# A two-block transformer kernel whose linear-attention loop takes its last two sequences one at a time

## The chip, the cores and the metric

The kernel runs on one core of a Trainium2 chip. The metric is the device time of one launch in microseconds. TensorE multiplies matrices into PSUM banks, VectorE and ScalarE work on SBUF and PSUM, GpSimd on SBUF alone, and SyncE issues the DMAs of the weights and of the output. The engines run beside each other and wait for one another through semaphores.

## The reference

x has 16 sequences of 128 tokens and 128 features, all float32. The first block is a conditioned transformer layer (16 heads of 8 features, RoPE, softmax attention, a gated feed-forward layer). The second, which the change touches, is linear attention. Cut to what matters:

```
xn = layer_norm(x)                      # x: output of the first block
q, k, v = xn@Wq+bq, xn@Wk+bk, xn@Wv+bv  # 16 heads of 8
q = softmax(q over the 8 features of a head)
k = softmax(k over the 128 tokens)
y = q @ (k^T v)  per head
h = layer_norm(y)*g*(1+scale)+shift     # scale, shift from cond
out = x + cond * (silu(h)@out_W + out_b)
```

Each sequence is independent of the others in the second block, so how many go together is free.

## The kernel before, in words

The first block works on sequences one by one (attention, to about 128 us) and then on pairs (feed-forward). UNIT is 2, U is 8, and `pair(u)` is the slice of pair u. The second block is a pipeline written out by hand: each engine has a function or loop body for a step t, and in step t it works on several pairs at different depths (`u = t - 3`, `u = t - 6` and so on). There are CD_STEPS = U + 9 steps. The order of the instructions of one engine in a step is the order of its program, each with waits on semaphores that count pairs. An engine never passes a waiting instruction, and buffers are doubled by `u % 2`.

The names that follow are used for the instructions; a number in brackets is the pair (or part).

- GpSimd (`blocks_gpsimd`), in its order in a step: qs (L509, q minus its maximum), res (L514, the result, for `t - 8`), then for `t - 5` nmr (L519, pairs below DRAIN alone), var (L481) and the power rstd (L483, in `std`) and nmr again (L523), then xs3 (L528, x times its inverse deviation, for t).
- ScalarE (`blocks_scalar`): kx (L580, two exponentials), qvb (L589, copy of q and v), qxT (L599), qe (L605), hT4 (L536, two, modulated layer norm of y) and th (L613, tanh), kxT (L618), xs4 (L624, two, normalised y, below DRAIN alone).
- VectorE (`c_step` in `blocks_vector`): qrec (L687), qmax (L693), hs (L699, for `t - 6`), bn (L705, two, for `t - 4`), krec (L711), mv (L716, two), cx (L723, two, for `t - 3`), xs (L733, two, for `t - 4` and from pair DRAIN on), gated (L742, output times cond, for `t - 6`), hT (L748), kmax (L752), qsum (L757), knb (L762), y (L768, for `t - 3`).
- TensorE (`c_step` in `blocks_tensor`): ctx (L852, k^T v, for `t - 3`), xd (transposes of xs, `t - 5`), qe transposed (`t - 3`), out (L875 and L876, output projection, `t - 6`), xc (transposes of xs3, t), K (L892), Y (L901, `t - 3`), kT (transposes of kx, `t - 2`), QV (L920, L921, for t). All transposes go through a helper at L786.
- SyncE (L964 to L967): for each pair one store of 128 KB after res, then a wait for all.

DRAIN is U - 2 = 6, so xs of pairs 6 and 7 is made by VectorE, which waits for the power of the same pair. kT and out share PSUM bank 0. Two waits keep them apart, in TensorE's program:

```
e.wait_ge(c_kxT, min(u + 4, U))   # before out(u)
wait(e, d_gated, u - 3)           # before kT(u)
```

Of the kernel before, what the change touches and what calls it, by code (L numbers as in the profile page):

```python
# [29 lines left out]
ACT = mybir.ActivationFunctionType  # L30
# [41 lines left out]
CD_STEPS = U + 9  # L72
# [19 lines left out]
def is_unit(u):  # L92
    return not isinstance(u, int) or 0 <= u < U


def dit_then_linear_attention(nc, x, cond, pos, norm1_w, qkv_w, q_norm_w, k_norm_w, proj_w, proj_b,
# [3 lines left out]
    with ctx:  # L100
# [339 lines left out]
        def blocks_gpsimd(g):  # L440
# [37 lines left out]
            def std(u, ready, mv, var, added, rstd, made):  # L478

                g.wait_ge(ready, u + 1)  # L480
                q.tensor_scalar(var[:, pair(u)], mv[:, pair(u), 1], 1.0, EPS1, ALU.mult, ALU.add).then_inc(added, 1)  # L481
                g.wait_ge(added, u + 1)
                q.tensor_tensor(rstd[:, pair(u)], var[:, pair(u)], minus_half[:, 0:UNIT], ALU.pow).then_inc(made, 1)  # L483

            def std2(u):
                if is_unit(u):
                    std(u, b_mv, mv2, var2, c_var, rstd2, c_rstd)
# [12 lines left out]
            for t in c_range():  # L500
# [5 lines left out]
                if is_unit(u):  # L506
                    g.wait_ge(c_qmax, u + 1)
                    wait(g, c_qe, u - 1)
                    q.tensor_tensor(qs[u % 2][:, :, :, :], qvb[u % 2][:, :, 0:D].rearrange("p u (h d) -> p u h d", d=DH),  # L509
                                    qmax[u % 2][:, :, :].unsqueeze(3).to_broadcast([128, UNIT, H, DH]), ALU.subtract).then_inc(c_qs, 1)  # L510
                u = t - 8
                if is_unit(u):
                    g.wait_ge(d_gated, u + 1)
                    q.tensor_tensor(res[:, pair(u), :], gated[u % 2][:, :, :], x2[:, pair(u), :], ALU.add).then_inc(s_res, 1)  # L514
                u = t - 5
                if is_unit(u):
                    g.wait_ge(c_mv, u + 1)
                    if u < DRAIN:
                        q.tensor_scalar(nmr3[:, pair(u)], mv3[:, pair(u), 0], -1.0, 0.0, ALU.mult, ALU.add)  # L519
                    std(u, c_mv, mv3, var3, d_var, rstd3, d_rstd)  # L520
                    if u < DRAIN:
                        g.wait_ge(d_rstd, u + 1)
                        q.tensor_tensor(nmr3[:, pair(u)], nmr3[:, pair(u)], rstd3[:, pair(u)], ALU.mult).then_inc(d_nmr, 1)  # L523
                u = t
                if is_unit(u):
                    g.wait_ge(c_rstd, u + 1)
                    wait(g, c_xsT, u - 1)
                    q.tensor_tensor(xs3[u % 2][:, :, :], x2[:, pair(u), :], wide(rstd2, u), ALU.mult).then_inc(c_xs, 1)  # L528

        def blocks_scalar(a, start=None):  # L530
# [39 lines left out]
            for t in c_range():  # L570
                u = t
                if u == 0:
                    a.wait_ge(c_xsT, u + 1)
                    q.activation(flat(hT3[u % 2]), bank[XC_BANK][:, 0:UNIT * T], ACT.Copy).then_inc(c_hT, 1)
                u = t - 2
                if is_unit(u):
# [7 lines left out]
                if is_unit(u):  # L584
# [4 lines left out]
                    q.activation(qvb[u % 2][:, :, 0:2 * D], bank[QV_BANK][:, :].rearrange("p (u f) -> p u f", f=2 * D),  # L589
                                 ACT.Copy).then_inc(c_qvb, 1)  # L590
                u = t
                if 0 < u < JOIN:
                    a.wait_ge(c_xsT, u + 1)
                    q.activation(flat(hT3[u % 2]), bank[XC_BANK][:, 0:UNIT * T], ACT.Copy).then_inc(c_hT, 1)
                u = t - 3
                if is_unit(u):
                    a.wait_ge(c_qxTp, u + 1)
                    wait(a, c_yp, u - 1)
                    q.activation(flat(qxT[u % 2]), bank[QT_BANK][:, 0:UNIT * T], ACT.Copy).then_inc(c_qxT, 1)  # L599
                u = t - 2  # L600
                if is_unit(u):
# [3 lines left out]
                    q.activation(qe[u % 2][:, :, :, :].rearrange("p u h d -> p (u h d)"),  # L605
                                 qs[u % 2][:, :, :, :].rearrange("p u h d -> p (u h d)"), ACT.Exp).then_inc(c_qe, 1)
                u = t - 5
                if is_unit(u):
                    a.wait_ge(d_xsT, u + 1)
                    wait(a, d_hs, u - 1)  # L610
                    modulated(hT4, u, u % 2, bank[XD_BANK], S3, A3).then_inc(d_hT, 1)
                    a.wait_ge(d_hT, u + 1)
                    q.activation(th4[u % 2][:, :], flat(hT4[u % 2]), ACT.Tanh, scale=0.5).then_inc(d_th, 1)  # L613
                u = t - 2
                if is_unit(u):
                    a.wait_ge(c_kxTp, u + 1)
                    wait(a, c_ctx, u - 1)
                    q.activation(flat(kxT[u % 2]), bank[KT_BANK][:, 0:UNIT * D], ACT.Copy).then_inc(c_kxT, 1)  # L618
                u = t - 4
                if is_unit(u) and u < DRAIN:  # L620
                    a.wait_ge(d_nmr, u + 1)
                    wait(a, d_xsT, u - 1)
                    for j in range(UNIT):
                        last = q.activation(xs4[u % 2][:, j, :], y[:, UNIT * u + j, :], ACT.Identity,  # L624
                                            bias=nmr3[:, UNIT * u + j:UNIT * u + j + 1], scale=rstd3[:, UNIT * u + j:UNIT * u + j + 1])
                    last.then_inc(d_xs, 1)

        def blocks_vector(v, start=None):
# [53 lines left out]
            def c_step(t):  # L682
                u = t - 3
                if is_unit(u):
                    v.wait_ge(c_qsum, u + 1)
                    wait(v, c_y, u - 1)
                    q.reciprocal(qrec[u % 2][:, :, :].rearrange("p u h -> p (u h)"),  # L687
                                 qsum[:, :, :].rearrange("p u h -> p (u h)")).then_inc(c_qrec, 1)
                u = t - 2
                if is_unit(u):  # L690
                    v.wait_ge(c_qvb, u + 1)
                    wait(v, c_qs, u - 1)
                    q.tensor_reduce(qmax[u % 2][:, :, :], qvb[u % 2][:, :, 0:D].rearrange("p u (h d) -> p u h d", d=DH),  # L693
                                    X_AXIS, ALU.max).then_inc(c_qmax, 1)
                u = t - 6
                if is_unit(u):
                    v.wait_ge(d_th, u + 1)
                    wait(v, d_op, u - 1)
                    q.scalar_tensor_tensor(hs[u % 2][:, :], th4[u % 2][:, :], 1.0, flat(hT4[u % 2]), ALU.add,  # L699
                                           ALU.mult).then_inc(d_hs, 1)  # L700
                u = t - 4
                if is_unit(u):
                    v.wait_ge(c_y, u + 1)
                    for j in range(UNIT):
                        last = q.bn_stats(bn3[:, UNIT * u + j, :], y[:, UNIT * u + j, :])  # L705
# [3 lines left out]
                if is_unit(u):  # L709
                    v.wait_ge(c_ctx, u + 1)  # L710
                    q.reciprocal(krec[:, :], ctx_[:, :, D:D + 1].rearrange("p u a -> p (u a)")).then_inc(c_krec, 1)  # L711
                u = t - 4
                if is_unit(u):
                    v.wait_ge(c_bn, u + 1)
                    for j in range(UNIT):
                        last = q.bn_aggr(mv3[:, UNIT * u + j, :], bn3[:, UNIT * u + j, :])  # L716
                    last.then_inc(c_mv, 1)
                u = t - 3
                if is_unit(u):
                    v.wait_ge(c_krec, u + 1)  # L720
                    wait(v, c_yp, u - 1)
                    for j in range(UNIT):
# [4 lines left out]
                if is_unit(u) and u >= DRAIN:  # L727
# [3 lines left out]
                    for j in range(UNIT):  # L731
                        b = UNIT * u + j
# [4 lines left out]
                if is_unit(u):  # L737
# [4 lines left out]
                    q.tensor_tensor(gated[u % 2][:, :, :], bank[OUT_BANK][:, 0:UNIT * D].rearrange("p (u f) -> p u f", f=D),  # L742
                                    gate[:, pair(u), :], ALU.mult).then_inc(d_gated, 1)
                u = t
                if is_unit(u) and u >= JOIN:
                    v.wait_ge(c_xsT, u + 1)
                    wait(v, c_k, u - 1)
                    q.tensor_copy(flat(hT3[u % 2]), bank[XC_BANK][:, 0:UNIT * T]).then_inc(c_hT, 1)  # L748
                u = t - 1
                if is_unit(u):  # L750
                    v.wait_ge(c_k, u + 1)
                    q.tensor_reduce(kmax[:, :], bank[K_BANK][:, 0:UNIT * T].rearrange("p (u t) -> p u t", t=T),  # L752
                                    X_AXIS, ALU.max, negate=True).then_inc(c_km, 1)
# [27 lines left out]
        def blocks_tensor(e, start=None):  # L781
# [61 lines left out]

            def c_step(t):
                u = t - 3
                if is_unit(u):
# [4 lines left out]
                    for j in range(UNIT):  # L851
# [4 lines left out]
                if is_unit(u):  # L856
# [4 lines left out]
                    turned(bank[XD_BANK], lambda j: xs4[u % 2][:, j, :], d_xsT)  # L861
                u = t - 3
                if is_unit(u):
                    e.wait_ge(c_qe, u + 1)
                    wait(e, c_qxT, u)
                    turned(bank[QT_BANK], lambda j: qe[u % 2][:, j, :, :].rearrange("p h d -> p (h d)"), c_qxTp)
                u = t - 6
                if is_unit(u):
# [3 lines left out]
                    e.wait_ge(c_kxT, min(u + 4, U))  # L872
                    for j in range(UNIT):
# [5 lines left out]
                if is_unit(u):  # L879
# [4 lines left out]
                    turned(bank[XC_BANK], lambda j: xs3[u % 2][:, j, :], c_xsT)  # L884
                u = t - 1
                if is_unit(u):
# [5 lines left out]
                    q.matmul(bank[K_BANK][:, 0:UNIT * T], linc[:, 2, :], flat(hT3[u % 2]), start=True, stop=True).then_inc(c_k, 1)  # L892
                u = t - 3
                if is_unit(u):
# [5 lines left out]
                    for j in range(UNIT):  # L900
# [3 lines left out]
                if is_unit(u):  # L904
# [5 lines left out]
                    turned(bank[KT_BANK], lambda j: kx[u % 2][:, j, :], c_kxTp)  # L910
                u = t
                if is_unit(u):
# [5 lines left out]
                    for j in range(UNIT):  # L918
# [1050 lines left out]
```

## Time and profile before

| | |
|---|---|
| runs | 212.53, 212.80, 213.04 us; median 212.8 |
| profiled execution | 211.97 us, span 210.2, mean granted clock 0.987 |
| busy (share of span) | TensorE 183.4 (87%), VectorE 164.0 (78%), ScalarE 130.7 (62%), GpSimd 135.9 (65%) |
| second block's loop | from about 161 us to the end |
| output | eight stores of 128.0 KB, median 1.8 us from issue to landing |

A timeline row gives the start in us from the span's start, the length in us, the engine, the line, the operation, the tile written and those read, the shapes and how many instructions were merged; in brackets how long the engine had been idle and who ended that. In the rows by stretch each engine has its busy time with the number of instructions, then come TensorE's granted clock (1.00 is 2.4 GHz, 0.50 is 1.2 GHz), the share of the DMA engines and GB/s; the order is TensorE's matmuls, its weight loads, VectorE, ScalarE, GpSimd. Consecutive starts on a full engine lie closer than the lengths, since the end of one overlaps the next.

### The profile page before, as it was taken

The page shows a single profiled execution, that of the slowest core. Times are in us where ns is not written, and L with a number is a line of the kernel's source. Part 1 is how long each engine was busy: PE and PEld are TensorE (multiplying, and loading weights), DVE is VectorE, ACT ScalarE, POOL GpSimd, SP SyncE. Part 2 cuts the span into 40 slices and gives each one's busy share as a digit, 9 for nine tenths or more (in the row PEclk, how much of TensorE's full clock was granted, in tenths as well). Part 3 has the DMA queues.
Part 4 walks back from the last instruction along what each step waited for, and adds up shares of the span by engine and source line. Part 5 has one row for each costly group of instructions (what it writes and reads, how often), then busy time and mean ns, then how long its engine had stood idle before and what let it go on. Part 6 is the DMA issues. An engine that isn't in the chain of part 4 may idle for free.

```text
span 210.2 us, 5867 instructions
## 1 busy us (share of the span) xinstructions
PE 183.4 (87%) x1986; PEld 141.1 (67%) x1986; DVE 164.0 (78%) x488; ACT 130.7 (62%) x354; POOL 135.9 (65%) x346
## 2 busy tenths in 40 slices
PE   1796868889999999899999999999998799998742
PEld 1544556667777777777776787788886478887522
DVE  4798898897979799996666434778899589999851
ACT  1476696677777777676555784453432367999740
POOL 8889798989786867758800783167512546757642
PEclk9999999999999999999999999999999999999995
DMA  5963000000000000000000000000000000001102
GB/s 111 280 178 142 0 5 3 0 0 3 3 3 2 3 6 0 3 3 2 3 3 0 3 3 0 2 0 0 6 0 0 0 2 3 0 25 30 51 26 74
DMA packets 9915, 5.13 MB, mean 24 GB/s; under 512 B 3025, under 2 KB 9758, under 8 KB 9758
## 3 DMA queue, kind: packets, MB, share of 16 engines
q1 hardware_dynamic: 6494, 4.08, 6.4%
q10 hardware_dynamic: 3392, 0.68, 1.6%
q8 instruction: 16, 0.26, 0.5%
q14 instruction: 13, 0.11, 0.2%
HBM read 3.71 MB, written 1.05 MB: 23 GB/s over the span
## 4 chain that ended last, share of the span: by engine, by line
PE 61%; DVE 21%; ACT 6%; issue 6%; POOL 2%; ACTq 2%; POOLq 0%; DVEq 0%
PE bank L1769 8%; DVE qkpad L1500 8%; PE bank L1778 7%; PE bank L1860 6%; PE bank L799 5%; PE bank L810 5%; PE bank L800 5%; PE bank L786 4%; PE bank L920 3%; PE bank L1801 2%; PE bank L1837 2%; PE bank L1872 2%; PE bank L852 2%; ACT probs L1201 2%; PE bank L1830 2%
## 5 line engine op out<-in xcount | busy, mean ns | idle before, releaser
L1201 ACT ACTIVATE probs<-bank 128x512 f32<-128x512 f32 x64 | 34.7, 594 | 22.6 <-PE bank L1778 22.5
L1500 DVE TENSOR_REDUCE qkpad<-bank 128x4 f32<-128x512 f32 x64 | 41.0, 684 | 9.1 <-PE bank L1769 7.7
L1778 PE MATMUL bank<-qTm,kBD 32*128 32x128 f32 x512 | 37.1, 283 | 0.4 <-ACT probs L1201 0.4
L1769 PE MATMUL bank<-kBD,qTs 32*128 32x256 f32 x224 | 31.7, 399 | 5.7 <-DVE qkpad L1500 4.2
L1778 PEld LDWEIGHTS bank<-qTm,kBD 32*128 32x128 f32 x512 | 31.0, 186 | 1.0 <-ACT probs L1201 0.6
L1769 PEld LDWEIGHTS bank<-kBD,qTs 32*128 32x128 f32 x224 | 19.8, 184 | 10.8 <-DVE qkpad L1500 7.4
L545 ACT ACTIVATE th<-bank 128x256 f32<-128x256 f32 x24 | 9.2, 384 | 18.9 <-PE bank L800 15.5
L1860 PE MATMUL bank<-probs,vpad 128*32 128x128 f32 x512 | 18.5, 277 | 0.2
L1051 POOL TENSOR_TENSOR partner<-qk,rope 128x96 f32<-128x96 f32 x32 | 14.3, 467 | 6.7 <-ACT qk L1243 6.7
L1801 PE MATMUL bank<-ident,qkpad 128*128 128x128 f32 x96 | 16.5, 281 | 0.8 <-DVE qkpad L1598 0.8
L481 POOL TENSOR_SCALAR var<-mv 128x2 f32<-128x2 f32 x16 | 3.1, 193 | 20.3 <-DVE mv L672 18.4
L1801 PEld LDWEIGHTS bank<-ident,qkpad 128*128 128x128 f32 x96 | 10.6, 141 | 7.2 <-issue 5.3
L1860 PEld LDWEIGHTS bank<-probs,vpad 128*32 128x32 f32 x512 | 12.6, 109 | 4.1 <-issue 2.0
L536 ACT ACTIVATE hT<-bank,mods 128x128 f32<-128x128 f32 x32 | 12.9, 459 | 2.9 <-PE bank L786 2.9
L799 PE MATMUL bank<-hT,w1T 128*128 128x256 f32 x48 | 14.5, 383 | 0.0
L1837 PE MATMUL bank<-qkvT,hT 128*128 128x384 f32 x32 | 14.5, 545 | 0.0
L800 PE MATMUL bank<-hT,w3T 128*128 128x256 f32 x48 | 14.3, 379 | 0.0
L810 PE MATMUL bank<-ff,w2T 128*128 128x256 f32 x48 | 12.9, 381 | 0.0
L786 PE MATMUL bank<-ident,xs 128*128 128x128 f32 x48 | 9.5, 280 | 3.0 <-DVE xs L733 1.8
L483 POOL TENSOR_TENSOR rstd<-var,minus_half 128x2 f32<-128x2 f32 x16 | 11.2, 699 | 1.3
L635 DVE SCALAR_TENSOR_TENSOR yg<-th,bank 128x256 f32<-128x256 f32 x24 | 10.0, 417 | 2.5 <-ACT th L545 2.2
L1062 POOL TENSOR_TENSOR rot<-qk,rope 128x256 f32<-128x256 f32 x16 | 11.6, 728 | 0.0
(250 smaller groups left out, 512.3 us busy)
## 6 DMA issues: line engine op xcount, KB each, us to landing
gate<-in_cond_dram SPq DMA_DIRECT2D x1, 1024.0 KB, 4.6
out_dram<-res SPq DMA_DIRECT2D x8, 128.0 KB, 1.8
xin<-in_x_dram ACTq DMA_DIRECT2D x2, 256.0 KB, 5.1
xin<-in_x_dram SPq DMA_DIRECT2D x1, 512.0 KB, 4.9
ada_n<-in_L_cond_ada_w_dram SPq DMA_DIRECT2D x1, 256.0 KB, 5.2
w_n<-in_L_cond_w_dram SPq DMA_DIRECT2D x2, 128.0 KB
qkv_n<-in_L_cond_qkv_w_dram SPq DMA_DIRECT2D x1, 192.0 KB, 3.9
w_n<-in_L_cond_w_dram SPq DMA_DIRECT2D x1, 170.5 KB
```

What stands on the lines that cost most here:

```text
L786: last = q.transpose(dst[:, j * 128:(j + 1) * 128], src(j), ident[:, :])
L799: q.matmul(bank[GU_BANK[c]][:, 0:UNIT * T], w1T[:, c * 128:c * 128 + 128], flat(hT2[1 - p]), start=True, stop=True)
L800: q.matmul(bank[GU_BANK[c]][:, UNIT * T:], w3T[:, c * 128:c * 128 + 128], flat(hT2[1 - p]), start=True, stop=True).then_inc(b_gu, 1)
L810: last = q.matmul(bank[F_BANK][:, 0:UNIT * T], w2T[:, c, :], ff[c][:, :], start=c == 0, stop=c == FC - 1)
L1051: last = q.tensor_tensor(heads(partner[b % 2][:, :, :])[:, :, :, k::2], heads(qk[b % NQK][:, :, :])[:, :, :, 1 - k:ROPE:2], table(b, 1)[:, ...
L1201: q.activation(probs[2 * r + i][:, :, :, :].rearrange("p f a t -> p (f a t)"), bank[E_BANK[i]][:, :], ACT.Exp, scale=SCALE).then_inc(s_p, 1)
L1500: q.tensor_reduce(out_, score_bank(b, r, i)[:, :].rearrange("p (f a t) -> p f a t", f=2, a=2), X_AXIS, ALU.max, negate=True).then_inc(s_ma ...
L1769: last = q.matmul(bank[S_BANK[i]][:, f * 2 * T:(f + 1) * 2 * T], qTs[b % 2][rows, f, :], kBD[b % NKB][rows, f, :, :].rearrange("p a t -> p ...
L1778: last = q.matmul(bank[E_BANK[i]][:, (2 * f + k) * T:(2 * f + k + 1) * T], kBD[t % NKB][rows, f, k, :], qTm[t % 2][rows, f, :], start=True ...
L1801: last = q.transpose(dst[:, at_ + f * T:at_ + (f + 1) * T], qkpad[b % NKB][:, s, 8 * f:8 * f + 8, :].rearrange("p h d -> p (h d)"), ident[ ...
L1837: q.matmul(front_bank(b)[:, 128:512], hT[b % 2][:, :], qkvT[:, :], start=True, stop=True).then_inc(s_qkv, 1)
L1860: last = q.matmul(bank[O_BANK][32 * c:32 * c + 32, r * T:(r + 1) * T], vpad[b % NVP][:, col:col + VSTEP], probs[2 * r + i][:, f, k, :], st ...
```

## The change

The second block's loop goes over nine parts in place of eight pairs. Parts 0 to 6 are the pairs 0 to 6; part 7 is sequence 14 alone and part 8 is sequence 15 alone. Each instruction of part 7 or 8 works on half the columns, groups of two instructions become one, and each of the two is stored by itself with 64 KB. There are 18 steps instead of 17. The offsets, the orders within a step, the banks and the buffers stay; DRAIN and JOIN keep their values, so parts 6, 7 and 8 have xs on VectorE. Everything ahead of the loop stays.

```diff
+C_UNITS = U + UNIT - 1
+CD_STEPS = C_UNITS + 9
+def is_part(u):
+    return not isinstance(u, int) or 0 <= u < C_UNITS
+def c_size(u):
+    return UNIT if u < U - 1 else 1
+def c_rows(u):
+    first = UNIT * u if u < U - 1 else UNIT * (U - 1) + u - (U - 1)
+    return slice(first, first + c_size(u))
...
-            def std(u, ready, mv, var, added, rstd, made):
+            def std(u, rows, ready, mv, var, added, rstd, made):
...
-                q.tensor_tensor(rstd[:, pair(u)], var[:, pair(u)], minus_half[:, 0:UNIT], ALU.pow).then_inc(made, 1)
+                q.tensor_tensor(rstd[:, rows], var[:, rows], minus_half[:, 0:rows.stop - rows.start], ALU.pow).then_inc(made, 1)
...
-                if is_unit(u):
-                    g.wait_ge(c_rstd, u + 1)
+                if is_part(u):
+                    g.wait_ge(c_rstd, min(u + 1, U))
...
-                if is_unit(u):
+                if is_part(u):
                     v.wait_ge(c_y, u + 1)
-                    for j in range(UNIT):
-                        last = q.bn_stats(bn3[:, UNIT * u + j, :], y[:, UNIT * u + j, :])
+                    for j in range(c_size(u)):
+                        last = q.bn_stats(bn3[:, c_rows(u).start + j, :], y[:, c_rows(u).start + j, :])
...
-                    e.wait_ge(c_kxT, min(u + 4, U))
-                    for j in range(UNIT):
+                    e.wait_ge(c_kxT, min(u + 4, C_UNITS))
+                    for j in range(c_size(u)):
...
                     wait(e, d_gated, u - 3)
-                    turned(bank[KT_BANK], lambda j: kx[u % 2][:, j, :], c_kxTp)
+                    turned_part(u, bank[KT_BANK], lambda j: kx[u % 2][:, j, :], c_kxTp)
...
-            for u in range(U):
+            for u in range(C_UNITS):
                 sp.wait_ge(s_res, u + 1)
-                sp.dma_start(out[pair(u), :, :].rearrange("b t f -> t b f"), res[:, pair(u), :]).then_inc(stored, 16)
-            sp.wait_ge(stored, 16 * U)
+                sp.dma_start(out[c_rows(u), :, :].rearrange("b t f -> t b f"), res[:, c_rows(u), :]).then_inc(stored, 16)
+            sp.wait_ge(stored, 16 * C_UNITS)
```

The other edits are of the same form: `is_unit` becomes `is_part`, `pair(u)` becomes `c_rows(u)`, a loop over UNIT becomes one over `c_size(u)`, and a tile is cut to its first `c_size(u)` entries.

## Rows read from the trace of the kernel before

**Rows 1.** Busy time by stretch; after the colon the length, then each engine.

```profile
187.30:191.00 3.70, 3.70 (x30) 3.31 (x29) 3.70 (x16) 3.67 (x12) 2.51 (x6) 1.00 0.13 40
202.00:206.00 4.00, 2.10 (x12) 1.57 (x12) 2.02 (x6) 1.23 (x3) 1.80 (x3) 0.84 0.11 33
```

**Rows 2.** VectorE's timeline, step 7; columns: start, length, line, operation, tiles, shapes.

```profile
187.12 0.41 DVE L748 COPY hT<-bank 128x256 f32<-128x256 f32 x1
187.45 0.41 DVE L752 TENSOR_REDUCE kmax<-bank 128x2 f32<-128x256 f32 x1
```

**Rows 3.** ScalarE's timeline, step 8.

```profile
190.21 0.38 ACT L599 ACTIVATE qxT<-bank 128x256 f32<-128x256 f32 x1
190.48 0.42 ACT L605 ACTIVATE qe<-qs 128x256 f32<-128x256 f32 x1
```

**Rows 4.** Groups by line and shape; count, then busy us and mean ns.

```profile
L1254 ACT ACTIVATE vpad<-bank 128x128 f32<-128x128 f32 x16 | 4.6, 288 | 0.0
...
L1519 DVE TENSOR_TENSOR o<-bank,rsum 128x128 f32<-128x128 f32 x16 | 4.5, 282 | 0.1
...
L1042 POOL TENSOR_TENSOR xs<-xin,rstd_x 128x128 f32<-128x128 f32 x8 | 3.2, 402 | 0.1
...
L483 POOL TENSOR_TENSOR rstd<-var,minus_half 128x2 f32<-128x2 f32 x16 | 11.2, 699 | 1.3
...
L1018 POOL TENSOR_TENSOR rstd_x<-ms,minus_half 128x4 f32<-128x4 f32 x2 | 2.0, 1025 | 0.5 <-DVE ms L1409 0.5
```

**Rows 5.** VectorE's timeline from mv(6) to the end.

```profile
196.88 0.23 DVE L716 BATCH_NORM_AGGREGATE mv<-bn 128x2 f32<-128x6 f32 x2
...
198.29 0.60 DVE L733 TENSOR_SCALAR xs<-y,mv,rstd 128x128 f32<-128x128 f32 x2 [0.68 <-POOL rstd L483]
198.81 0.42 DVE L742 TENSOR_TENSOR gated<-bank,gate 128x256 f32<-128x256 f32 x1
...
199.47 0.84 DVE L699 SCALAR_TENSOR_TENSOR hs<-th,hT 128x256 f32<-128x256 f32 x1
...
200.23 0.47 DVE L705 BATCH_NORM_STATS2 bn<-y 128x6 f32<-128x128 f32 x2
...
202.17 0.60 DVE L733 TENSOR_SCALAR xs<-y,mv,rstd 128x128 f32<-128x128 f32 x2 [1.18 <-POOL rstd L483]
...
204.41 0.42 DVE L742 TENSOR_TENSOR gated<-bank,gate 128x256 f32<-128x256 f32 x1 [0.97 <-PE bank L876]
204.75 0.41 DVE L699 SCALAR_TENSOR_TENSOR hs<-th,hT 128x256 f32<-128x256 f32 x1
...
206.79 0.42 DVE L742 TENSOR_TENSOR gated<-bank,gate 128x256 f32<-128x256 f32 x1 [1.63 <-PE bank L876]
```

**Rows 6.** GpSimd's timeline of the drain.

```profile
195.91 0.93 POOL L514 TENSOR_TENSOR res<-gated,x 128x256 f32<-128x256 f32 x1
...
197.27 0.19 POOL L481 TENSOR_SCALAR var<-mv 128x2 f32<-128x2 f32 x1 [0.43 <-DVE mv L716]
...
199.31 0.72 POOL L514 TENSOR_TENSOR res<-gated,x 128x256 f32<-128x256 f32 x1 [1.05 <-DVE gated L742]
...
207.30 0.72 POOL L514 TENSOR_TENSOR res<-gated,x 128x256 f32<-128x256 f32 x1 [1.55 <-DVE gated L742]
```

**Rows 7.** TensorE's timeline: ctx(7), first output matmuls of pairs 6 and 7.

```profile
196.05 0.71 PE L852 MATMUL bank<-qvb,kxT 128*128 128x129 f32 x4 [0.56 <-ACT kxT L618]
...
203.49 0.49 PE L875 MATMUL bank<-outw,hs 128*128 128x128 f32 x2 [0.22 <-DVE hs L699]
...
205.22 0.79 PE L875 MATMUL bank<-outw,hs 128*128 128x128 f32 x2 [0.85 <-DVE hs L699]
```

**Rows 8.** Busy time by stretch at the end, with granted clock and DMA share.

```profile
204.50:205.00 0.50, 0.00 (x0) 0.00 (x0) 0.50 (x2) 0.06 (x1) 0.09 (x1) 0.74 0.07 23
...
209.00:209.25 0.25, 0.00 (x0) 0.00 (x0) 0.00 (x0) 0.00 (x0) 0.00 (x0) 0.50 1.08 328
209.25:209.50 0.25, 0.00 (x0) 0.00 (x0) 0.00 (x0) 0.00 (x0) 0.00 (x0) 0.50 0.55 156
```

More of the change, by code:

```diff
@@ L511, in blocks_gpsimd @@
                 u = t - 8
-                if is_unit(u):
+                if is_part(u):
                     g.wait_ge(d_gated, u + 1)
-                    q.tensor_tensor(res[:, pair(u), :], gated[u % 2][:, :, :], x2[:, pair(u), :], ALU.add).then_inc(s_res, 1)
+                    q.tensor_tensor(res[:, c_rows(u), :], gated[u % 2][:, 0:c_size(u), :], x2[:, c_rows(u), :], ALU.add).then_inc(s_res, 1)
                 u = t - 5
-                if is_unit(u):
+                if is_part(u):
                     g.wait_ge(c_mv, u + 1)
@@ L609, in blocks_scalar @@
                     a.wait_ge(d_xsT, u + 1)
                     wait(a, d_hs, u - 1)
-                    modulated(hT4, u, u % 2, bank[XD_BANK], S3, A3).then_inc(d_hT, 1)
+                    rows = c_rows(u)
+                    for j in range(c_size(u)):
+                        b = rows.start + j
+                        last = q.activation(hT4[u % 2][:, j, :], bank[XD_BANK][:, j * T:(j + 1) * T], ACT.Identity,
+                                            bias=mods[:, b, S3:S3 + 1], scale=mods[:, b, A3:A3 + 1])
@@ L612, in blocks_scalar @@
+                    last.then_inc(d_hT, 1)
                     a.wait_ge(d_hT, u + 1)
-                    q.activation(th4[u % 2][:, :], flat(hT4[u % 2]), ACT.Tanh, scale=0.5).then_inc(d_th, 1)
+                    q.activation(th4[u % 2][:, 0:c_size(u) * T], flat(hT4[u % 2])[:, 0:c_size(u) * T], ACT.Tanh, scale=0.5).then_inc(d_th, 1)
                 u = t - 2
-                if is_unit(u):
+                if is_part(u):
                     a.wait_ge(c_kxTp, u + 1)
                     wait(a, c_ctx, u - 1)
-                    q.activation(flat(kxT[u % 2]), bank[KT_BANK][:, 0:UNIT * D], ACT.Copy).then_inc(c_kxT, 1)
+                    q.activation(flat(kxT[u % 2])[:, 0:c_size(u) * D], bank[KT_BANK][:, 0:c_size(u) * D], ACT.Copy).then_inc(c_kxT, 1)
@@ L619, in blocks_scalar @@
                 u = t - 4
-                if is_unit(u) and u < DRAIN:
+                if is_part(u) and u < DRAIN:
                     a.wait_ge(d_nmr, u + 1)
                     wait(a, d_xsT, u - 1)
-                    for j in range(UNIT):
-                        last = q.activation(xs4[u % 2][:, j, :], y[:, UNIT * u + j, :], ACT.Identity,
-                                            bias=nmr3[:, UNIT * u + j:UNIT * u + j + 1], scale=rstd3[:, UNIT * u + j:UNIT * u + j + 1])
+                    for j in range(c_size(u)):
+                        b = c_rows(u).start + j
+                        last = q.activation(xs4[u % 2][:, j, :], y[:, b, :], ACT.Identity,
+                                            bias=nmr3[:, b:b + 1], scale=rstd3[:, b:b + 1])
@@ L726, in c_step @@
                 u = t - 4
-                if is_unit(u) and u >= DRAIN:
+                if is_part(u) and u >= DRAIN:
                     v.wait_ge(d_rstd, u + 1)
@@ L730, in c_step @@
                     v.wait_ge(d_xs, u)
-                    for j in range(UNIT):
-                        b = UNIT * u + j
+                    for j in range(c_size(u)):
+                        b = c_rows(u).start + j
                         last = q.tensor_scalar(xs4[u % 2][:, j, :], y[:, b, :], mv3[:, b, 0:1], rstd3[:, b:b + 1], ALU.subtract,
@@ L741, in c_step @@
                         v.wait_ge(ld_gate, 16)
-                    q.tensor_tensor(gated[u % 2][:, :, :], bank[OUT_BANK][:, 0:UNIT * D].rearrange("p (u f) -> p u f", f=D),
-                                    gate[:, pair(u), :], ALU.mult).then_inc(d_gated, 1)
+                    n = c_size(u)
+                    q.tensor_tensor(gated[u % 2][:, 0:n, :], bank[OUT_BANK][:, 0:n * D].rearrange("p (u f) -> p u f", f=D),
+                                    gate[:, c_rows(u), :], ALU.mult).then_inc(d_gated, 1)
@@ L842, in blocks_tensor, with turned_part @@
                 return b_first, b_input, b_rest
+            def turned_part(u, dst, src, sm):
+                for j in range(c_size(u)):
+                    last = q.transpose(dst[:, j * 128:(j + 1) * 128], src(j), ident[:, :])
+                last.then_inc(sm, 1)
             def c_step(t):
                 u = t - 3
-                if is_unit(u):
+                if is_part(u):
                     e.wait_ge(c_kxT, u + 1)
@@ L850, in c_step @@
                     wait(e, c_cx, u)
-                    for j in range(UNIT):
+                    for j in range(c_size(u)):
                         last = q.matmul(bank[CTX_BANK][:, j * (D + 1):(j + 1) * (D + 1)], kxT[u % 2][:, j, :],
@@ L883, in c_step @@
                     wait(e, c_hT, u)
-                    turned(bank[XC_BANK], lambda j: xs3[u % 2][:, j, :], c_xsT)
+                    turned_part(u, bank[XC_BANK], lambda j: xs3[u % 2][:, j, :], c_xsT)
                 u = t - 1
-                if is_unit(u):
+                if is_part(u):
                     e.wait_ge(c_hT, u + 1)
@@ L899, in c_step @@
                         e.wait_ge(b_fg, U)
-                    for j in range(UNIT):
+                    for j in range(c_size(u)):
                         last = q.matmul(bank[Y_BANK][:, j * D:(j + 1) * D], qxT[u % 2][:, j, :], cx[u % 2][:, j, :], start=True, stop=True)
@@ L917, in c_step @@
                         e.wait_ge(c_bias, 6)
-                    for j in range(UNIT):
+                    for j in range(c_size(u)):
                         dst = bank[QV_BANK][:, j * 2 * D:(j + 1) * 2 * D]
```

132 lines of the change are left out of this document (71 added, 61 removed).

## The prediction

> **What bounds the kernel now.** A name with a number is an instruction of that part: hs(7) is the one that makes hs of part 7, with the lines of the section on the kernel. I read the busy shares by stretch first. Around step 8 the loop is full on three engines: VectorE is busy 3.70 of 3.70 us, ScalarE 3.67 and TensorE 3.70; from 202 us on none is (TensorE 2.10 of 4.00, VectorE 2.02, ScalarE 1.23) [rows 1]. So the loop is bound by throughput to about 194 us and after that by one chain of handovers, which the timelines give. The chain is: the aggregate mv(6) at 196.88, then POOL's var(6) at 197.27 and its power, then xs(6) at 198.29; the same loop for pair 7 ends in xs(7) at 202.17, 3.88 us later; then transposes, hT4, th, hs(7) at 204.75, the output projection at 205.22, gated(7) at 206.79, res(7) at 207.30 to 208.02 and the last store [rows 5 to 7]. xs(7) to the end of res(7) is 5.85 us.
>
> The profiled execution took 211.97 us for a span of 210.2; the median of the runs is 212.8, 0.83 above it. I add my difference to both. A measurement of this kernel can tell about 0.2%, 0.43 us, from no change.
>
> **The price of a half.** On VectorE a start follows a start after 0.33 us with 256 columns (187.12 to 187.45) [rows 2]; a pair of bn or xs, 128 columns each, lasts 0.47 or 0.60 [rows 5], so I take 0.20 for a copy, a product or a bn of 128 and 0.26 for xs, an estimate; a lone 128-column instruction lasts 0.28 from start to landing and a 256-column one 0.41 [rows 2, 4]. ScalarE copies: 0.38 for 256 columns, 0.29 for 128 [rows 3, 4]. GpSimd: 0.72 for 256 [rows 6], 0.40 for 128, and I take 0.45 for two full operands. Its power takes 0.70 for 2 columns and 1.03 for 4 [rows 4], 0.16 a column, so 0.54 for one. On TensorE a half costs a half. Over the whole loop a pair cut in two costs VectorE about 0.8 us more (twelve instructions with some 0.07 each beyond their columns) and ScalarE about 0.4.
>
> On ScalarE the two rows with 256 columns start 0.27 us apart (190.21, 190.48) [rows 3], so I charge no more than 0.2 for a half in the full part of the loop. The Trainium skill (VectorE: DVE Perf Modes, on the TRN2 errata) gives ScalarE a fixed term of 224 cycles for operands in SBUF, 0.40 us for 256 columns and 0.29 for 128; by it the change would lose about 0.1 more per ScalarE step, but the trace's spacing is below what it says.
>
> **Steps 7 to 9: little changes.** xs3, the transposes, hT, K and QV of part 7 halve in step 7 and those of part 8 come in step 8. Walking the orders of the queues with the spacings above, by my sums VectorE starts step 8 about 0.12 us earlier and step 9 about 0.2 earlier. QV(8), 0.55 us on TensorE, lies in the time in which TensorE now waits for kxT(6), as it waits 0.56 for kxT(7) ahead of ctx(7) [rows 7]. In step 9 and 10 the gain is lost again: y(6) waits for Y(6), which waits for cx(6), and VectorE now also does kmax(8), knb(8), qmax(8). I get mv(6) ending at 196.93 against 197.11. On GpSimd, qs(8) (0.45) now stands ahead of res(3), which took 0.93 from 195.91 [rows 6]: qmax(8) ends near 195.95, qs(8) near 196.46, res(3) near 197.2, and only then comes var(6). The two meet: var(6) at 197.15 to 197.4 against 197.27, and xs(6) at 198.3 as now. Bounds: 0.18 earlier if res(3) takes 0.72, 0.2 later if it again takes 0.93. I take 0.
>
> **Link 7.** VectorE stands in xs(6) until 198.3, so gated(4) starts at 198.81 and ends at 199.23, as now [rows 5]. New is who waits: bank 0 is shared by kT and the output, so kT(8) waits for gated(4); it runs 199.27 to 199.54, kxT(8) to 199.85, and ctx(8), half of a group that takes 0.71 for a pair [rows 7], to 200.35. xd(6), qe(8) and out(5) are queued behind ctx(8) on TensorE; out(5) also waits by its own rule for kxT(8). On VectorE y(7) takes 0.20, hs(5) is stretched as now (it took 0.84 from 199.47 while res(4) ran on GpSimd from 199.31) [rows 5, 6], bn(7) starts at 200.23 as now but is one instruction, krec(8) at 200.43, mv(7) ends 200.70; var(7), the power of one column (0.54): xs(7) at 201.72, 0.45 before now.
>
> **Link 8, which is new.** xs(7) 0.26, gated(5) 0.33, y(8) 0.20: hs(6) at 202.51. If it runs in 0.33, bn(8) is at 202.84, mv(8) ends 203.29, var(8) starts 203.45, the power 203.73 to 204.28, xs(8) 204.32: a link of 2.60 us. But res(5) starts on GpSimd at 202.48, as close ahead of hs(6) as res(4) was of hs(5), which then ended 0.28 after the end of res(4); so hs(6) would end at 203.5 and xs(8) start at 204.87. ScalarE's queue does not bound this: qxT(8), hT4(6) and th(6), late because xd(6) stands behind ctx(8), end near 202.3. The two bounds are 204.32 and 204.87.
>
> **The end.** From xs(8): gated(6) after 0.20, hs(7) at +0.54, landed at +0.82. Then out(7). TensorE's granted clock has fallen by then: it averages 0.74 from 204.5 to 205.0 [rows 8], where TensorE is idle between two output projections, so it goes from the 2.4 to the 1.2 GHz level there; the first pair of output matmuls takes 0.79 instead of 0.49, and 1.57 us pass from it to gated(7) [rows 5, 7]. One sequence I put at 0.89. gated(7) stands ahead of hs(8) on VectorE, so hs(8) (its th(8) is ready at +1.5) starts at +2.0 and lands at +2.28; out(8) 0.89 more, gated(8) with 0.28, res(8) with 0.45 and four handovers of 0.04 to 0.09: res(8) ends 4.08 us after xs(8), where it was 5.85 after xs(7). The end of res(8) is thus 208.40 or 208.95, against 208.02 now: +0.38 or +0.93. The last store is 64 KB instead of 128: the DMA engines were busy 1.08 and 0.55 of two quarters of a microsecond with the last one [rows 8], 0.41 us, half of that is saved: -0.2. The eighth store goes out over 1 us earlier and is covered. **The sum:** +0.18 to +0.73, I take +0.45: a span of 210.65, and 213.3 for the median.
>
> **Rivals.**
> *A, faster: the clock holds.* out(7) and out(8) run at the 2.4 GHz level. A pair of them took from 203.49 to the start of gated(6) at 204.41 there [rows 5, 7], so one takes 0.5: twice 0.39 is saved, and with the short link 8 the time is 212.8 + 0.18 - 0.78 = 212.2. It decides at one place: whether the gap ahead of out(7) still leaves the full level. For it: TensorE gets kT(8), ctx(8) and Y(8) more between 199 and 202. Against it: these are halves, and xd(8) and out(7) again stand in gaps. The Trainium skill (Perfetto Trace Analysis, Optimizing Scalar/DVE Operations) says that breaking up instructions may let work finish sooner where these engines only cause bubbles for others; the stretch after 202 us is such a place, so it speaks for this side. 17%.
> *B, slower by more: the new link costs what a link costs now.* 3.88 us twice puts xs(8) at 206.06 and res(8) at 210.14: 214.7; one link of 3.43 and one like it puts xs(8) at 205.15: 213.8. For it: in each link VectorE runs in order, and one late hs, bn or krec holds all behind it. Against it: bn, mv and the power do halve. Middle 214.3, 15%.
> *C, no change:* var(6) escapes GpSimd's queue (0.18 earlier) and the short link holds: 212.8 + 0.18 - 0.18 = 212.8, or the clock holds but the link is long, 212.75. 20%.
> *My forecast*, 213.0 to 213.5: 48%, and of it a quarter lies within 0.43 us of 212.8.
>
> **How the numbers follow.** Faster by over 0.2%: 17%. Within: 20 and 13, 33%. Slower: 35 and 15, 50%. The range from 212.1 to 214.3 takes in the forecast, C, most of A and the lower half of B. The forecast's own range is 213.0 to 213.5.
>
> **What would show it.** Right: xs(6) near 198.3; kT(8) starting just after gated(4), near 199.3; three xs on VectorE spaced 3.4 and 2.6 to 3.1 us; gated(7) ahead of hs(8) with the clock at 0.50; res(8) at 0.45 us ending about 4.1 us after xs(8). Wrong: xs(6) earlier than 198.0 (the first halves gained more than I credit), a third xs more than 3.4 us after the second (B), a granted clock of 1.00 in the last output matmuls (A), or hs(6) in 0.41 us, which leaves the short sum.

## The result, and the profile after

The changed kernel took 213.87 us (median of 6 executions, 212.67 to 214.22) against 212.67 for the kernel before (6, 212.47 to 213.21): a ratio of 1.0042, 95% interval 1.0022 to 1.0063, so slower by 0.5 to 1.3 us. Its profiled execution took 212.67, the lowest of the six, with a span of 211.0 against 210.2.

The busy shares by stretch, to compare with [rows 1], and the place where TensorE's granted clock (third number from the end) falls:

```profile
187.30:191.00 3.70, 3.58 (x28) 2.98 (x27) 3.70 (x17) 3.67 (x12) 2.94 (x8) 1.00 0.12 35
202.00:206.00 4.00, 3.02 (x11) 1.73 (x10) 2.47 (x9) 1.55 (x5) 2.25 (x5) 0.50 0.11 33
201.00:201.50 0.50, 0.50 (x7) 0.48 (x6) 0.34 (x2) 0.39 (x2) 0.22 (x2) 1.00 0.66 202
201.50:202.00 0.50, 0.50 (x5) 0.48 (x2) 0.00 (x0) 0.50 (x2) 0.50 (x1) 0.51 0.22 61
```

The throughput part hardly changed: VectorE and ScalarE are as full as before. From 202 to 206 us TensorE looks busier, 3.02 for 2.10, but it does no more: there are 11 records of matmuls for 12, and its clock is at 0.50 where it averaged 0.84 before. It fell at 201.5, and at about 204.75 before [rows 8].

VectorE's timeline in the drain, which answers to [rows 5]:

```profile
198.51 0.60 DVE L762 TENSOR_SCALAR xs<-y,mv,rstd 128x128 f32<-128x128 f32 x2 [1.14 <-POOL rstd L500]
199.02 0.42 DVE L772 TENSOR_TENSOR gated<-bank,gate 128x256 f32<-128x256 f32 x1
...
199.91 0.62 DVE L727 SCALAR_TENSOR_TENSOR hs<-th,hT 128x256 f32<-128x256 f32 x1
...
202.07 0.35 DVE L762 TENSOR_SCALAR xs<-y,mv,rstd 128x128 f32<-128x128 f32 x1 [0.72 <-POOL rstd L500]
...
202.86 0.42 DVE L727 SCALAR_TENSOR_TENSOR hs<-th,hT 128x256 f32<-128x256 f32 x1
...
204.81 0.35 DVE L762 TENSOR_SCALAR xs<-y,mv,rstd 128x128 f32<-128x128 f32 x1 [1.12 <-POOL rstd L500]
205.07 0.42 DVE L772 TENSOR_TENSOR gated<-bank,gate 128x256 f32<-128x256 f32 x1
205.41 0.28 DVE L727 SCALAR_TENSOR_TENSOR hs<-th,hT 128x128 f32<-128x128 f32 x1
206.68 0.29 DVE L772 TENSOR_TENSOR gated<-bank,gate 128x128 f32<-128x128 f32 x1 [0.99 <-PE bank L915]
206.89 0.28 DVE L727 SCALAR_TENSOR_TENSOR hs<-th,hT 128x128 f32<-128x128 f32 x1
208.16 0.29 DVE L772 TENSOR_TENSOR gated<-bank,gate 128x128 f32<-128x128 f32 x1 [0.99 <-PE bank L915]
```

There are three xs, and VectorE waits ahead of each for GpSimd's power (`rstd`). A link is the way from one xs to the next, through y, bn, mv, var and the power: 198.51 to 202.07 is 3.56 us (link 7), 202.07 to 204.81 is 2.74 (link 8), where one link of 3.88 stood. Then gated(7) at 206.68 stands ahead of hs(8) at 206.89, and the last gated comes at 208.16.

GpSimd's timeline, which answers to [rows 6]:

```profile
196.21 0.51 POOL L527 TENSOR_TENSOR qs<-qvb,qmax 128x128 f32<-128x128 f32 x1 [0.68 <-DVE qmax L720]
196.69 0.72 POOL L532 TENSOR_TENSOR res<-gated,x 128x256 f32<-128x256 f32 x1
197.49 0.19 POOL L498 TENSOR_SCALAR var<-mv 128x2 f32<-128x2 f32 x1
...
202.82 1.03 POOL L532 TENSOR_TENSOR res<-gated,x 128x256 f32<-128x256 f32 x1 [0.79 <-DVE gated L772]
203.94 0.19 POOL L498 TENSOR_SCALAR var<-mv 128x1 f32<-128x1 f32 x1
204.22 0.56 POOL L500 TENSOR_TENSOR rstd<-var,minus_half 128x1 f32<-128x1 f32 x1
...
208.53 0.45 POOL L532 TENSOR_TENSOR res<-gated,x 128x128 f32<-128x128 f32 x1 [1.02 <-DVE gated L772]
```

qs(8) and res(3) stand ahead of var(6). res(5), 1.03 us long beside hs(6), ends at 203.85, and var(8) waits for it although mv(8) was done at 203.69 (0.18 from 203.51). That costs about 0.1 us, since var(7) also started 0.16 us after the end of its mv. The last res ends at 208.98, 0.96 later than before.

TensorE's timeline, with the gap that is new:

```profile
197.61 0.44 PE L941 MATMUL bank<-cx,qxT 128*128 128x128 f32 x2
199.59 0.30 PE L880 MATMUL bank<-ident,kx 128*128 128x128 f32 x1 [1.54 <-DVE gated L772]
...
203.33 0.80 PE L914 MATMUL bank<-outw,hs 128*128 128x128 f32 x2 [0.38 <-DVE hs L727]
```

kT(8) stands behind Y(7) in TensorE's order. Its input kx(8) is done at 196.8, but it waits to 199.59 for gated(4), and TensorE is idle for 1.54 us. The output matmuls of pair 6 take 0.80 in place of 0.49 [rows 7].

### The profile page after: what moved, and what is told of

Read it like the earlier page. It is cut to its first block, busy times and chain, and to the rows that moved or that the text cites. A ratio compares the mean times of both kernels' runs of the same rounds, so it can differ in the third digit from the quotient of the medians.

```text
span 211.0 us, 5920 instructions
## 1 busy us (share of the span) xinstructions
PE 185.1 (88%) x1988; PEld 142.1 (67%) x1988; DVE 164.7 (78%) x498; ACT 131.6 (62%) x359; POOL 136.8 (65%) x351
## 3 DMA queue, kind: packets, MB, share of 16 engines
q1 hardware_dynamic: 6510, 4.08, 6.4%
## 4 chain that ended last, share of the span: by engine, by line
PE 58%; DVE 23%; issue 6%; ACT 5%; POOL 4%; ACTq 2%; POOLq 0%; DVEq 0%
PE bank L1809 8%; DVE qkpad L1540 8%; PE bank L1818 7%; PE bank L1900 6%; PE bank L833 5%; PE bank L844 5%; PE bank L834 5%; PE bank L960 2%; PE bank L1841 2%; PE bank L1877 2%; PE bank L880 2%; PE bank L820 2%; PE bank L1912 2%; ACT probs L1241 2%; PE bank L1870 2%
## 5 line engine op out<-in xcount | busy, mean ns | idle before, releaser
L498 POOL TENSOR_SCALAR var<-mv 128x2 f32<-128x2 f32 (+1 forms) x17 | 3.3, 192 | 19.9 <-DVE mv L697 18.4
L500 POOL TENSOR_TENSOR rstd<-var,minus_half 128x2 f32<-128x2 f32 (+1 forms) x17 | 11.6, 681 | 1.4
L1153 POOL TENSOR_TENSOR qkpad<-rot,ny 128x256 f32<-128x256 f32 x15 | 9.7, 647 | 2.2 <-DVE ny L1632 0.4
L1585 DVE TENSOR_TENSOR x<-bank,xin 128x128 f32<-128x128 f32 x16 | 4.7, 292 | 7.8 <-PE bank L1870 7.8
```

Of the source, the lines that this page charges most:

```text
L500: q.tensor_tensor(rstd[:, rows], var[:, rows], minus_half[:, 0:rows.stop - rows.start], ALU.pow).then_inc(made, 1)
```

## The experiments

Two theories: **L**, the loss is the added link through y, bn, power and xs; **K**, it is the clock, which the gap ahead of kT(8) lets fall early. They do not exclude each other. Ratios are to the kernel before, run on the same chip, with 95% intervals. xs(6) to the end of the last res is a length inside one profile: 9.73 us in the kernel before, 10.47 in the changed one.

**The changed kernel again.** No edit.

> The changed kernel once more, unedited, for a second profile beside the edits that follow. The profiled execution of the first measurement, 212.67 us, was the fastest of six and the median was 213.87. Theory K (the wait of kT(8) for gated(4) empties TensorE for 1.5 us and the clock falls early): in a typical execution the clock falls before 201.5 us, perhaps inside that gap, and the part from xs(7) to the end is longer than the 6.9 us of the first profile; the time is 213.6 to 214.1. Theory L (the extra link alone): the clock's fall is where it was and any longer time comes from before 196 us.

Median 213.44, ratio 1.0043 (1.0026 to 1.0059). Its profiled execution was again the fastest (212.46), and its clock falls at about 205.2 us, not before 201.5; that part of the expectation was missed, and the median is below its 213.6 to 214.1:

```profile
204.00:205.00 1.00, 0.00 (x0) 0.00 (x1) 0.40 (x2) 0.00 (x0) 0.56 (x1) 1.00 0.42 126
205.00:206.00 1.00, 0.83 (x3) 0.61 (x4) 0.48 (x2) 0.57 (x2) 0.64 (x1) 0.58 0.02 5
```

Its links are 3.55 and 2.75 us, the whole length 10.48: with the fall at 201.5 or at 205.2 the length is the same, since the two last output projections run at the lower level in both. But every execution has a mean clock. Of this kernel's twelve, nine were at 0.966 to 0.973 with spans of 211.6 to 212.5, three at 0.977 to 0.987 with 210.7 to 211.2; 28 of the kernel before beside them were at 0.975 to 0.987, with a median span of 210.9. So the changed kernel's median differs from its profiled execution by the clock. With like mean clocks (0.978) the spans of the two kernels are 211.0 and about 210.9; why they are alike, although a link was added, comes out under the store alone.

**Own bank for kT(8).**

```diff
-                    wait(e, d_gated, u - 3)
-                    turned_part(u, bank[KT_BANK], lambda j: kx[u % 2][:, j, :], c_kxTp)
+                    if u < C_UNITS - 1:
+                        wait(e, d_gated, u - 3)
+                    turned_part(u, bank[KT_BANK if u < C_UNITS - 1 else XC_BANK], lambda j: kx[u % 2][:, j, :], c_kxTp)
...
-                    e.wait_ge(c_kxT, min(u + 4, C_UNITS))
+                    e.wait_ge(c_kxT, min(u + 4, C_UNITS - 1))
```

(kxT(8) reads from the same bank.)

> kT(8) goes to the transposes' bank 7, which nothing uses by then, so neither kT(8) waits for gated(4) nor out(5) for kxT(8). Theory K: TensorE has no gap of 1.5 us, kT(8) starts near 198.0, the clock falls later than 201.5, and the time is 0.4 to 1.0 us below the changed kernel. Theory L: krec(8) and ctx(8) come earlier but xs(7) still waits for hs(5), bn(7) and the power; the time is 0 to 0.2 below the changed kernel.

Median 212.57, ratio 1.0001 (0.9991 to 1.0012): the median's whole loss is gone. Its profile:

```profile
203.00:203.50 0.50, 0.13 (x1) 0.00 (x0) 0.50 (x3) 0.33 (x1) 0.34 (x1) 0.73 0.00 0
...
198.02 0.44 PE L941 MATMUL bank<-cx,qxT 128*128 128x128 f32 x2
198.30 0.27 PE L880 MATMUL bank<-ident,kx 128*128 128x128 f32 x1
199.44 0.49 PE L891 MATMUL bank<-qvb,kxT 128*128 128x129 f32 x2 [0.88 <-ACT kxT L642]
...
203.66 0.80 PE L914 MATMUL bank<-outw,hs 128*128 128x128 f32 x2 [0.53 <-DVE hs L727]
```

kT(8) follows Y(7) at once; the longest gaps there are now 0.88 and 0.74 us for 1.54. But link 7 shortened by 0.09 us only (198.93 to 202.40), and the length is 10.40. The gain is in the clock, which fell at about 203.2 here: eight of eleven executions were at 0.978 to 0.989 with spans of 210.7 to 210.9, a ninth, the profiled one, at 0.981 with 211.3 and its xs(6) 0.4 us later. This favours K for the median. It does not say that the added link is free.

**The power first.** In GpSimd's step 11 `res` was moved behind the block with var and rstd.

> In GpSimd's step 11 res(3) stands behind var(6) and the power of 6 in place of ahead of them. If the queue behind qs(8) is what puts xs(6) at 198.51 in place of 198.29, var(6) starts near 197.3, xs(6) near 198.3, and the time is 0.2 below the changed kernel. If VectorE's mv(6) were the limit nothing changes. res(3) must not hold anything: res(4) starts only at 199.5.

Median 213.89, ratio 1.0049 (1.0034 to 1.0063): no gain. var(6) did come at 197.25, but res(3) then ran beside xs(6):

```profile
198.26 1.00 DVE L766 TENSOR_SCALAR xs<-y,mv,rstd 128x128 f32<-128x128 f32 x2 [0.93 <-POOL rstd L500]
```

1.00 in place of 0.60 us, so the 0.24 gained were lost. The profile is of the other kind, with the fall inside the gap; the length is 12.07 us, with links of 4.40 and 3.49:

```profile
198.00:199.00 1.00, 0.00 (x0) 0.00 (x0) 0.74 (x2) 0.73 (x2) 0.91 (x2) 1.00 0.00 0
199.00:199.50 0.50, 0.00 (x0) 0.00 (x0) 0.50 (x2) 0.00 (x0) 0.00 (x0) 0.69 0.00 0
199.50:200.00 0.50, 0.27 (x1) 0.18 (x1) 0.50 (x4) 0.00 (x0) 0.34 (x1) 0.50 0.28 87
```

TensorE is idle until kT(8) comes, the clock falls at about 199.2, and then kT(8), ctx(8), out(5) and Y(8) lie in the links at 1.2 GHz. Its mean clock, 0.969, and its span, 212.3, are those of most executions of the changed kernel, of which none was profiled.

**Filled.** Idle transposes of the identity into a free bank, in the changed kernel and in the kernel before:

```diff
+            def fill(n):
+                for _ in range(n):
+                    q.transpose(bank[XC_BANK][:, 0:128], ident[:, :], ident[:, :])
```

The edits place them a little otherwise than the two expectations say: in the changed kernel 12 ahead of kT(8), 3 after xd(7), 2 after out(6) and 4 after out(7); in the kernel before 6 after xd(6), 10 after out(5) and 6 after out(6).

> The changed kernel with idle transposes of the identity into the free bank 7 on TensorE: 12 ahead of kT(8), 2 and 4 after xd(7) and xd(8), 3 after out(6); the output does not use them. Theory K (the clock): the clock stays at the 2.4 GHz level through out(7) or out(8), each of which falls from 0.9 to about 0.5 us, and the time is 0.6 to 1.2 below the changed kernel, level with or below the kernel before. Theory L: the clock was no part of the loss, the time stays within 0.3 of the changed kernel.

> The kernel before with idle transposes of the identity into the free bank 7: 10 after xd(6), 6 after xd(7), 6 after out(5). If the clock costs the kernel before only what its last pair of output matmuls pays (1.57 us against 0.92 to the next gated), the time is 0.3 to 0.7 below the kernel before. If filling is worth more to the changed kernel (0.6% between it and its filled form) than to this one, the clock explains the difference between the two kernels; if both gain the same, it doesn't and the extra link does.

The filled changed kernel took 212.15 (ratio 0.9981, 0.9967 to 0.9996), 1.3 us less than unfilled beside it. The filled kernel before took 211.22 (0.9936, 0.9919 to 0.9953), 1.4 less. So the kernel before paid 1.4 us for the clock too, where I had seen only its last matmuls pay. By the medians the two gain the same, and by the rule of the expectation the link then explains the difference. But the filling does not hold the clock in every execution of the changed kernel: mean clocks are 0.986 to 1.000 there and 0.992 to 1.000 in the kernel before. At 0.999 to 1.000 the spans are 209.9 to 210.2 (four executions) and 209.4 to 209.5 (four). Against these most unfilled executions of the changed kernel (212.2) pay about 2.1 us and those of the kernel before (210.9) 1.4. So of the 1.3 us between their spans about 0.6 is the link and 0.7 the clock. With the clock at 1.00 through the last matmul of both the profiles differ by the same. xs(6) to the end of the last res:

```profile
198.39 0.60 DVE L762 TENSOR_SCALAR xs<-y,mv,rstd 128x128 f32<-128x128 f32 x2 [1.13 <-POOL rstd L500]
...
207.33 0.29 DVE L772 TENSOR_TENSOR gated<-bank,gate 128x128 f32<-128x128 f32 x1 [0.64 <-PE bank L921]
...
207.00:207.50 0.50, 0.29 (x3) 0.06 (x2) 0.17 (x1) 0.00 (x0) 0.03 (x1) 1.00 0.81 245
```

for the changed kernel, ending with res at 208.15, 9.76 us; and for the kernel before 9.07, from

```profile
198.19 0.60 DVE L733 TENSOR_SCALAR xs<-y,mv,rstd 128x128 f32<-128x128 f32 x2 [0.68 <-POOL rstd L483]
...
206.04 0.42 DVE L742 TENSOR_TENSOR gated<-bank,gate 128x256 f32<-128x256 f32 x1 [0.97 <-PE bank L882]
...
205.00:206.00 1.00, 0.88 (x6) 0.64 (x6) 0.07 (x1) 0.00 (x0) 0.65 (x1) 1.00 0.31 91
```

to 207.26. That is +0.69; in the unfilled profiles it was +0.74, where each kernel had paid about 0.7 for the clock. The spans are 210.1 and 209.5.

**Own bank and filled.** The bank edit with fewer idle transposes, 14 for 21, in the places that its expectation names.

> The changed kernel with kT(8) in bank 7 and idle transposes on TensorE: 5 ahead of out(5), 2 and 4 after xd(7) and xd(8), 3 after out(6). If the own bank helped by the clock alone (its links were only 0.1 us shorter), it adds little to the filled form: 211.9 to 212.3 against 212.15. If waiting for gated(4) had a price beyond the clock, 211.6 or below. Either way it stays 0.6 or more above the filled kernel before (211.22), because the extra link remains.

Median 212.09, ratio 0.9993 (0.9972 to 1.0014), within noise of the filled form. Own bank and filling do not add: both act through the clock. By the medians 0.87 us above the filled kernel before remain, as expected; four of these twelve executions were at 0.982 to 0.986, so some of that is still the clock, and the lengths at the full clock (9.69 for 9.07) put the link at 0.6.

**The store alone.** The kernel before with res(7) and its store in two.

> Eight pairs as before; only res(7) and its store are cut in two, nine stores in all. The part of the change that is the store alone: two res of 0.45 in place of one of 0.72, the first store 0.27 us earlier, the last one of 64 KB 0.2 us shorter but 0.18 later: within 0.2 of the kernel before. If the ninth store costs a descriptor's fixed time at the end, 0.3 or more slower.

212.58, ratio 0.9994 (0.9983 to 1.0006): no difference between nine stores and eight is seen. The chain up to gated(7) is that of the kernel before, and the profiled execution, at a mean clock of 0.980 with a span of 210.8, is like most of that kernel's. It shows what the profile at 0.987 did not:

```profile
202.00:203.00 1.00, 0.22 (x1) 0.23 (x2) 0.88 (x4) 0.00 (x0) 0.09 (x1) 0.77 0.00 0
203.00:204.00 1.00, 1.00 (x4) 0.59 (x4) 0.39 (x2) 0.50 (x2) 0.84 (x1) 0.50 0.00 0
...
205.02 0.42 DVE L747 TENSOR_TENSOR gated<-bank,gate 128x256 f32<-128x256 f32 x1 [1.63 <-PE bank L881]
205.36 0.41 DVE L704 SCALAR_TENSOR_TENSOR hs<-th,hT 128x256 f32<-128x256 f32 x1
207.41 0.42 DVE L747 TENSOR_TENSOR gated<-bank,gate 128x256 f32<-128x256 f32 x1 [1.64 <-PE bank L881]
```

The clock falls at about 202.5, in TensorE's idle time after out(5). gated(6) and with it hs(7) wait 1.63 us instead of 0.97 for out(6), and gated(7) again: from xs(6) to the last gated it is 9.17 us, 8.50 in the profile before and 7.85 filled. The kernel before pays for two whole pairs of output matmuls in its chain. In the changed kernel out(6) at the lower level delays nothing that follows (gated(6) starts right behind xs(8)), and only the two halves pay, about 0.35 us each (each out is waited for 0.99 us, 0.64 filled). So with the own bank, whose clock falls at 203.2, the added link and the smaller price of the clock about cancel, and the ratio is 1.0001.

**Halves without a link.** Eight pairs; only the last pair is cut, from xs(7) on and inside its own step.

```diff
+                if t - 5 == U - 1:
+                    u = U - 1
+                    wait(v, d_op, u - 1)
+                    for j in range(UNIT):
+                        v.wait_ge(d_th, U + j)
+                        q.scalar_tensor_tensor(hs[u % 2][:, j * T:(j + 1) * T], th4[u % 2][:, j * T:(j + 1) * T], 1.0,
+                                               hT4[u % 2][:, j, :], ALU.add, ALU.mult).then_inc(d_hs, 1)
```

That is VectorE's part, ahead of gated(6); the other engines' instructions for pair 7 become one for each sequence in the same way, in banks of their own. So the edit changes three things: the halves, the order of hs(7) and gated(6), and the banks.

> Eight pairs as before, but the last pair is cut in two only from xs(7) on, inside its own step: transposes, hT4, th, hs, out, gated, res and store by sequence, in banks 3, 7, 5 and 6, with hs(7) ahead of gated(6) on VectorE. No extra pass through y, bn, power. Theory L and K together: no link is added and TensorE has no new gap, the halves overlap, the last res ends 1.0 to 1.4 us earlier and the last store is 64 KB: 1.0 to 1.6 us below the kernel before, 211.1 to 211.7. If halves as such were what costs (fixed parts per instruction), it is at or above the kernel before.

211.01, ratio 0.9925 (0.9910 to 0.9941): 1.6 us below the kernel before, at the far end of what was expected. Its profile:

```profile
204.04 0.29 DVE L756 SCALAR_TENSOR_TENSOR hs<-th,hT 128x128 f32<-128x128 f32 x1 [0.59 <-ACT th L621]
204.66 0.29 DVE L756 SCALAR_TENSOR_TENSOR hs<-th,hT 128x128 f32<-128x128 f32 x1 [0.33 <-ACT th L621]
205.09 0.42 DVE L770 TENSOR_TENSOR gated<-bank,gate 128x256 f32<-128x256 f32 x1
205.79 0.29 DVE L763 TENSOR_TENSOR gated<-bank,gate 128x128 f32<-128x128 f32 x1 [0.28 <-PE bank L912]
206.37 0.29 DVE L763 TENSOR_TENSOR gated<-bank,gate 128x128 f32<-128x128 f32 x1 [0.28 <-PE bank L912]
```

The second half's hs is done before gated(6), so TensorE goes from out(6) to both halves of out(7) without a gap, and the halves follow each other 0.58 us apart, not 1.48 as in the changed kernel. The clock had fallen here too, at about 202.8. How much of the 1.6 us is the order alone is not shown. An estimate: in the profile of the store alone th(7) is done at 204.76 and hs(7) starts at 205.36, behind gated(6), so moving a whole hs(7) ahead could be worth up to 0.6.

**Both.** The same, filled with 17 idle transposes, with a wait for y(7) ahead of them.

> The last pair cut in halves from xs(7) on, plus idle transposes into bank 2 (free after y(7)): 4 ahead of out(5), 10 after it, 3 ahead of out(6). The profile of the tail in halves had the clock at 0.50 from 203 us, where out(6) and the two halves of out(7) take 2.6 us in a row. If the two gains are separate: 210.2 to 210.6. If GpSimd's three res in a row (0.72 + 0.92) are the bound at the end, filling brings less than 0.4: 210.7 or more.

210.75, ratio 0.9929 (0.9909 to 0.9949), the fastest median, 0.26 below the tail in halves, which was measured on another chip; the ratios do not separate the two. It is the expectation's second case, 210.7 or more. Its clock holds to the last matmul, and what ends last is GpSimd:

```profile
205.25 0.72 POOL L514 TENSOR_TENSOR res<-gated,x 128x256 f32<-128x256 f32 x1 [1.26 <-DVE gated L770]
205.93 0.86 POOL L519 TENSOR_TENSOR res<-gated,x 128x128 f32<-128x128 f32 x2
```

## Why the prediction was right, and where not

The wide range, 212.1 to 214.3, holds the measured 213.87; the forecast's own range, 213.0 to 213.5, does not. The direction and the added link are right, the size is half of it, and the wide range was wide enough through rival B, whose mechanism did not come in the changed kernel's profiles. That part is luck. By places ("the text" is the prediction):

- *Parity at xs(6)*: 198.51 in the profile, 198.30 in the second one, for 198.3. In both, xs(6) starts 1.62 us after mv(6), where it was 1.41 before. The queue of qs(8) and res(3) ahead of var(6) is there. That moving res(3) away gives 0.2 back was an assumption, and it fell: res beside xs costs more.
- *Link 7*: 3.56 us for 3.42. The wait is there (kT(8) at 199.59, 0.15 us after the end of gated(4), for 0.04 in the text). The excess is krec(8), at +2.28 from xs(6) for +2.13: it stands ahead of mv(7) on VectorE and waits for ctx(8) (200.26, 0.49), whose way through kT(8) and kxT(8) took 0.15 more than I summed. bn(7) is at +1.94 for +1.93.
- *Link 8*: 2.74, between the 2.60 and 3.15 of the text. hs(6) was not stretched (0.42), which the text had named as a sign that its short sum would hold; res(5) was (1.03), and its end bound var(8). The text expected the stretch on the other of the two, since res(5) starts first (202.82 and 202.86).
- *The end*: 4.17 us from xs(8) for 4.08, with gated(7) ahead of hs(8), 0.99 us of waiting for each out, and the clock at 0.50.
- *The sum*: +0.96 at the end of res for +0.38 to +0.93: the short sum's +0.38 and 0.21, 0.14, 0.14 and 0.09 from the four places above. The span is +0.8 for +0.45. The last store was busy 0.43 and 0.46 of two quarters, 0.22 us for 0.41, as forecast.
- *The clock* was the term mis-sized, on both sides. The text let it fall "by then" as before and asked only whether it would hold (A, which did not come). It did not ask whether the gap that it had itself found ahead of kT(8) would make it fall sooner. In most executions it seems to: the own bank takes the gap away and the low mean clocks nearly with it, but a fall inside the gap is seen only in the profile with GpSimd's edit. It adds about 1.2 us to the span (212.2 against 211.0 at mean clocks of 0.970 and 0.978). The median's loss is 1.2 us (0.9 by the ratio) for a forecast 0.5. One profiled execution of a kernel is one draw: the kernel before's 0.987 was the best of its own range too, and most of its executions, at about 0.978, are 0.7 us longer, since both of its last pairs of output matmuls pay.
- B's mechanism, a third link as long as the others, did not come in the two profiles of the changed kernel; with GpSimd's edit and the early fall, links of 4.40 (0.4 of it the stretched xs) and 3.49 are near it.

The trace agrees with what the text drew from the Trainium skill (Perfetto Trace Analysis, Optimizing Scalar/DVE Operations) only where the halves overlap: breaking up the last instructions, together with a changed order, won 1.6 us inside one step and lost as a step of its own. On the Trainium skill's fixed term for ScalarE (VectorE: DVE Perf Modes, on the TRN2 errata) the text read the wrong row: the term of 224 cycles is for operands in SBUF, and qxT reads a PSUM bank. qe reads SBUF, and hT4 follows it:

```profile
190.78 0.81 ACT L536 ACTIVATE hT<-bank,mods 128x128 f32<-128x128 f32 x2
...
197.37 0.30 ACT L624 ACTIVATE qe<-qs 128x128 f32<-128x128 f32 x1
197.57 0.80 ACT L633 ACTIVATE hT<-bank,mods 128x128 f32<-128x128 f32 x2
```

The first is from the kernel before, 0.30 us after its qe of 256 columns [rows 3], the others from the changed one, 0.20 us apart with 128. Both are below the 0.40 and 0.29 that the formula gives, so the text's conclusion stands; the lengths of qe, 0.42 and 0.30, are near the formula.

## What to carry to other kernels

Here a half of the work as a part of its own passed the slow loop once more and lost; cut after the last power, inside the step, with its own banks and its hs ahead of the other pair's gated, it won. So look first at what a new part has to pass again, and leave that whole. When a part is added to a hand-ordered pipeline, look for each wait written with a fixed distance (here gated, three parts behind) and ask what has meanwhile moved ahead of it. Read the mean clock of every execution beside the profiled one before taking its timeline as typical.

## What the runs showed of the hardware

The granted clock falls at quite different times in executions of one kernel: in the changed kernel at 201.5 and 205.2 us, and at 199.2 with an edit on GpSimd, at mean clocks from 0.966 to 0.987; in the kernel before at 204.7, and at 202.5 with the last store cut. Idle matmuls, 22 in all between 199 and 205 us, bring 1.4 us in the kernel before, whose output does not use them. What the lower level costs depends on what it meets: 0.7 us for each pair of output matmuls in the chain, nothing for one that is hidden.

When GpSimd's res of 256 columns runs beside VectorE's hs of 256 columns or its xs, one of the two is often stretched: hs from 0.41 to 0.62 or 0.84, res from 0.72 to 1.03, xs from 0.60 to 1.00. Which of the two paid did not follow from which started first. Other overlaps show nothing: bn(6) in the changed kernel took 0.48 beside res(3), which took 0.72.
